# One scalar step of the second normalisation moved ahead of two VectorE instructions in beat 5 of a Hyena and gated-FFN kernel

## The reference

```python
u  = x @ in_proj_w.T + in_proj_b            # 1536 columns, then a causal convolution of 3 taps
x0, x1, v = split(short_conv(u))
v  = fftconv(v * x1, k, filter_bias)        # long convolution; k comes from a small network
x  = layernorm(x + (v * x0) @ out_proj_w.T + out_proj_b)
h  = silu(x @ Wg.T) * (x @ Wu.T)            # 1408 hidden columns, dequantised integer weights
x  = layernorm(x + h @ Wd.T)
```

## Time and profile before

| | before |
|---|---|
| runs | 1001.90, 1002.41, 1002.76 us (median 1002.41) |
| profiled execution | 1001.72 us, span 999.9 us |
| TensorE busy | 972.3 us, 97% of the span |
| VectorE, GpSimd, ScalarE busy | 734.2, 570.5, 426.7 us |
| granted TensorE clock | 0.996 of 2.4 GHz as a mean |

### The profile page before, as it was taken

One profiled execution on the slowest core, in us unless ns is written; L12 is line 12 of the kernel. 1 busy time (PEld: TensorE's weight loads), 2 busy tenths in 40 slices (PEclk: granted clock), 3 DMA queues, 4 the chain that ended last, 5 costly groups with the idle time before them and its releaser, 6 DMA issues.

```text
span 999.9 us, 17201 instructions
## 1 busy us (share of the span) xinstructions
PE 972.3 (97%) x6188; PEld 761.7 (76%) x6188; DVE 734.2 (73%) x1345; ACT 426.7 (43%) x929; POOL 570.5 (57%) x628
## 2 busy tenths in 40 slices
PE   7999999999999999999999999999999999999996
PEld 5578777778777777778777787777877777787774
DVE  6598776868777787777878777876877777686454
ACT  4675534333353434434443343443335343434242
POOL 4589673755646476464656647465654747565210
PEclk9999999999999999999999999999999999999998
DMA  8654101121122101221102211112111110101100
GB/s 248 202 178 122 39 1 23 21 64 23 43 43 55 31 2 43 43 64 22 32 12 43 64 23 43 27 26 55 22 43 22 43 22 1 44 1 44 43 22 22
DMA packets 98952, 47.96 MB, mean 48 GB/s; under 512 B 80048, under 2 KB 84784, under 8 KB 98868
## 3 DMA queue, kind: packets, MB, share of 16 engines
q1 hardware_dynamic: 98370, 46.79, 18.0%
q10 hardware_dynamic: 498, 0.08, 0.0%
HBM read 32.17 MB, written 8.39 MB: 41 GB/s over the span
## 4 chain that ended last, share of the span: by engine, by line
PE 69%; DVE 13%; issue 6%; ACT 5%; POOL 4%; DMA 1%; ACTq 0%; POOLq 0%; SPq 0%; DVEq 0%
PE gate_up L1132 11%; PE gate_up L1133 11%; PE bank L992 9%; PE bank L994 9%; PE bank L993 9%; PE down L1144 5%; PE down L1145 5%; PE bank L1092 4%; DVE hid_lo L982 2%; DVE tmp L903 2%; ACT cx L675 2%; DVE cx L876 2%; PE bank L1067 1%; ACT x L700 1%; DVE cx L879 1%
## 5 line engine op out<-in xcount | busy, mean ns | idle before, releaser
L762 POOL TENSOR_TENSOR acc<-acc,tmp 128x256 f32<-128x256 f32 x160 | 123.3, 770 | 148.9 <-DVE tmp L903 136.9
L903 DVE TENSOR_TENSOR tmp<-spectrum,filt 128x512 f32<-128x512 f32 x256 | 172.6, 680 | 0.4 <-PE spectrum L994 0.4
L1132 PE MATMUL gate_up<-x2T_hi,wg_sb 128*128 128x256 f16 x704 | 163.4, 273 | 0.0
L1133 PE MATMUL gate_up<-x2T_lo,wu_sb 128*128 128x256 f16 x704 | 163.3, 273 | 0.0
L1133 PE MATMUL gate_up<-x2T_lo,wg_sb 128*128 128x256 f16 x704 | 163.3, 273 | 0.0
L1132 PE MATMUL gate_up<-x2T_hi,wu_sb 128*128 128x256 f16 x704 | 163.2, 273 | 0.0
L726 ACT ACTIVATE hid<-gate_up,gate_scale 128x256 f32<-128x256 f32 x176 | 82.7, 470 | 184.9 <-PE gate_up L1133 184.8
L756 POOL TENSOR_TENSOR acc<-acc,tmp 128x512 f32<-128x512 f32 x96 | 126.3, 1315 | 48.5 <-DVE tmp L903 48.0
L992 PE MATMUL bank<-xT_hi,win_hi 128*128 128x512 f32 x360 | 149.5, 415 | 1.4 <-POOL win_lo L744 1.2
L994 PE MATMUL bank<-xT_hi,win_lo 128*128 128x512 f32 x360 | 143.4, 398 | 0.0
L993 PE MATMUL bank<-xT_lo,win_hi 128*128 128x512 f32 x360 | 143.0, 397 | 0.0
(11 more groups left out here) (170 smaller groups left out, 1831.5 us busy)
## 6 DMA issues: line engine op xcount, KB each, us to landing
x<-in_x SPq DMA_DIRECT2D x28, 256.0 KB, 2.8
out<-x SPq DMA_DIRECT2D x28, 256.0 KB, 2.1
xstage<-in_x SPq DMA_DIRECT2D x96, 64.0 KB, 2.5
xstage<-in_x SPq DMA_DIRECT2D x12, 256.0 KB, 3.9
x<-in_win SPq DMA_DIRECT2D x12, 256.0 KB, 4.9
acc<-in_decay SPq DMA_DIRECT2D x4, 256.0 KB
x<-in_wout SPq DMA_DIRECT2D x4, 256.0 KB, 2.8
x2T_hi<-in_wu SPq DMA_DIRECT2D x4, 256.0 KB, 4.2
```

The lines of the kernel that those rows point to most:

```text
L762: G.tensor_tensor(acc[:, i, 0, :], acc[:, i, 0, :], t[:, 1, :], ALU.subtract)
L903: TT(dst, spectrum[j % 2][:, :, :], k_part, ALU.mult).then_inc(made_done, 1)
L1132: mm(dst, w[:, kb, rows(q)], x2T_hi[:, kb, ts], start=kb == 0, stop=False)
L1133: last = mm(dst, w[:, kb, rows(q)], x2T_lo[:, kb, ts], start=False, stop=kb == CB - 1)
```

## The change

In the passes in which beat 5 has both a half to finish (`done`) and a unit (`u`), the step `norm LN2` stands behind `hhi` of the unit, where it stood behind the second part of `mul`, `hlo` and `dn`. Passes n = 4 to 18 have both; n = 19 has no unit and stays.

```diff
     if u:
         steps += [("hmul", *u), ("hhi", *u)]
+        if beat == 5 and done:
+            steps += [("norm", LN2, n - 4)]
...
     if beat == 5 and done:
-        steps += [("norm", LN2, n - 4)]
+        if not u:
+            steps += [("norm", LN2, n - 4)]
         steps += [("store", n - 4, 0), ("store", n - 4, 1)]
```

## The result

| | before | after |
|---|---|---|
| median of 6 runs | 1002.15 us | 995.25 us (994.19 to 996.12) |
| ratio, 95% interval | | 0.9932 (0.9920 to 0.9944) |
| profiled execution, span | 1001.72, 999.9 us | 995.0, 993.2 us |

The account below looks back on a forecast made before the run. The prediction took TensorE's instructions plus its waits to bound the kernel. Steady passes -6.74, pass 16 +2.33 and pass 17 -0.56 gave -4.97 us, from 1002.41 to 997.4 us, range 994.8 to 1000.3.

Parts of the forecast that it names:

- The chain: Steady passes: TensorE's `op` waits for convolution L879, behind ScalarE's L675, behind normalisation L700, behind `shift`; all twelve waits go.
- The size of that term: Steady passes 4 to 15: twelve waits of TensorE removed in full, -6.74 us.
- every wait really costs 0.17 us more than its bracket: TensorE's waits: down products start 0.21 us apart but show as 0.38 long, so 12 x 0.17 joins 4.7 us.
- Hold of `shift`: VectorE, steady passes: moved `shift` lasts 0.58 us (bounds 0.15 and 1.23), delaying `mul` part 1 at no cost to TensorE.
- Pass 16: n = 16: `shift` waits for late `rstd` with `mul` part 1 and `hlo` queued behind, so `fw(15, 3)` starts late, +2.33 us.
- Pass 17: n = 17: normalisation of m = 13, its stores and reload come earlier, shortening TensorE's wait for `hlo`, -0.56 us.
- The sum: Whole kernel: -6.74 + 2.33 - 0.56 = -4.97 us, forecast 997.4 us, chance 0.50.
- The lower clock: Rival: TensorE's clock drops behind the new stall in pass 16, costing 1.70 us, 999.1 us; chance 0.21.
- Pass 16 costs nothing: Rival: GpSimd's backlog shrinks and `rstd` is early in pass 16, -7.3 us, 995.1 us; chance 0.09.
- The waits: Rival: another release takes over for `op`, half of the twelve waits left, -1.6 us, 1000.8 us; chance 0.12.
- The slower rival: `shift` holds `mul` part 1 until `fw(n-1, 3)` waits; with 4.5 us of hold +8.2 us, 1010.6 us; chance 0.03.

Follow-up runs that it names:

- e1: Against the kernel before: `shift` moved in the steady passes alone (n = 4 to 15), passes 16 and 17 in the old order; 994.73 us, ratio 0.9927.
- e4: Against the kernel before: `shift` of all fourteen places moved up by one instruction only, between `mul` part 1 and `hlo`; 994.62 us, ratio 0.9927.
- e3: Against the kernel before: VectorE's order kept, ScalarE's normalisation L700 put behind the convolution L675 in the steady passes; 994.02 us, ratio 0.9924.
- e8: e3 with `shift` of m = 13 (pass 17) moved as well; 994.39 us, ratio 0.9918 to the kernel before.
- e9: e1 with four extra VectorE instructions, output unused, behind each of the twelve moved `shift`s, 2.4 us of hold; 993.78 us, ratio 0.9920.
- e10: e1 with seven extra VectorE instructions, output unused, behind each of the twelve moved `shift`s, 4.2 us of hold; 1006.37 us, ratio 1.0049.
- e2: Against the kernel before: `shift` of m = 12 (pass 16) alone moved; 1004.49 us, ratio 1.0024.
- e7: Changed kernel, all fourteen places moved, with GpSimd computing `rstd` of m = 12 ahead of two additions; 993.78 us, ratio 0.9909.
- e6: Changed kernel with the old order for m = 12 (pass 16) alone; 993.66 us, ratio 0.9911.
- e11: The changed kernel measured and profiled once more, beside e12 on one chip; 995.52 us, ratio 0.9932.
- e12: The kernel of e7 measured and profiled once more, beside e11; 993.39 us, ratio 0.9915.
- e5: Against the kernel before: `shift` of m = 13 (pass 17) alone moved, one profile; 1002.84 us.

## Why the prediction was right, and where it was off

- **The chain.** TensorE's twelve waits came from L675 queued behind L700 behind `shift`. Shown from three sides: by moving `shift` (e1), by moving it less (e4), and by not moving it and reordering ScalarE (e3, e8). e1, e4 and e8 give -8.0 us in the steady stretch; of e3 there are only the times, with a ratio like theirs.
- **The size of that term** was forecast as 4.7 + 12 x 0.17 = 6.74 us and measured as 8.0. The step that failed is "every wait really costs 0.17 us more than its bracket". I took the loss up to the start of the first product and left out that this product then takes 0.33 us to the next one where 0.24 is usual. By the loads the gain is 0.77 us in pass 4, 0.81 to 0.83 in passes 5, 7, 9, 11 and 13, and 0.51 to 0.53 in the other six, 8.0 together.
- **Hold of `shift`**: taken 0.58 us out of a range from 0.15 to 1.23, measured 0.55 to 0.56 in eleven steady passes and 1.14 in the first. Its cost of nothing is right: 2.4 us more of it is free (e9), 4.2 us is not (e10). With `fw` 0.86 late behind 4.2 us of hold the cover is 3.3 us, against 3.4 in the prediction, which left out the 0.14 us from the end of `mul` to `fw`. One reading there was off: a `shift` that starts at 492.22 and ends near 494.0 lasts 1.78 us, 0.55 more than the upper bound of 1.23 and not "a little"; the bank would then be free 0.2 us ahead and not 0.8. In e4 `shift` does end there (490.73, or 494.0 in before's times), and the waits are gone all the same.
- **Pass 16**: forecast +2.33, measured +2.37 to +2.39, for the stated reason (e2, e7). What the sum did not have is what follows: 0.80 us come back at two waits of TensorE for `hlo` (0.41 at 913.7 and 0.39 at 920.3 us before). The expectations of e2 and e6 say that the stall gives them back, and the traces bear that out. The first of the two waits ends a chain on VectorE that begins when GpSimd's L779 releases L918; before, VectorE and TensorE:

```profile
907.32 0.69 DVE L918 TENSOR_TENSOR xstage<-bank,xstage 128x512 f32<-128x512 f32 x1 [4.05 <-POOL xstage L779]
...
912.95 0.72 DVE L982 TENSOR_TENSOR hid_lo<-hid,hid_hi 128x256 f16<-128x256 f32 x1
...
913.72 0.39 PE L1144 MATMUL down<-wd_sb,hid_hi 128*128 128x512 bf16 x1
```

TensorE's stall does not delay L918, so TensorE comes later to an `hlo` that is ready. In e4, where the stall is 1.26 us, this `hlo` ends at 905.88 us, to 0.01 where it was (913.67 before, less the 7.78 by which TensorE is ahead until pass 16), and the down product starts 1.0 us behind it without a wait:

```profile
905.16 0.72 DVE L984 TENSOR_TENSOR hid_lo<-hid,hid_hi 128x256 f16<-128x256 f32 x1
...
906.89 0.38 PE L1146 MATMUL down<-wd_sb,hid_hi 128*128 128x512 bf16 x1
```

With a stall of 2.38 us L918 stands where it was too, to 0.06 us (changed kernel, e2, e11). In e7 and e12 TensorE is only 0.45 us late, but L918 comes 0.58 us earlier (906.74 for 907.32 in before's times), and the two together again exceed 0.80. So at most the 0.80 us of these two waits can come back, whatever the stall. That some 0.25 us are lost there in e1, e5, e6, e8 and e9 has another cause: GpSimd's `rstd` of m = 12 lasts 0.98 us in these five and 0.71 before and in e10, and `shift` and the two waits end about 0.27 us later. It starts within 0.02 us of VectorE's `hlo`, which lasts 0.41 us in the five, 0.47 before and 0.46 in e10, so the same two instructions meet each time with a different outcome, in e5 too, where nothing ahead of them is changed.

- **Pass 17**: forecast -0.56; -0.44 and -0.35 in the changed kernel, and 0.49 between the means with and without it. The sign holds, and the chain up to the reload with 0.67 us (e5); the size of what reaches TensorE is blurred by the transfer.
- **The sum** by the profile: +0.15 - 8.01 + 2.37 - 0.80 - 0.44 = -6.73, and the spans differ by 6.7. The forecast of -4.97 is short by 1.3 in the first term and 0.8 in the second, and both errors go the same way. That the time still lies 0.45 us inside the range owes something to luck: its lower end of 994.8 was set for another case, a free pass 16, which did not come.
- **The rivals.** The lower clock did not come: behind the stall of 2.1 to 2.2 us the granted clock stayed at 1.00 in the three profiles that have it (changed kernel, e2, e11). "Pass 16 costs nothing" gave nearly the right time (995.1) for the wrong reason. The waits did not come back, and no other release took over (TensorE has no wait from 180 to 880 us). The slower rival's hold did not occur; e10 makes it by hand, and its 4.2 us of hold put the steady stretch 5.3 us above before.

The best kernels are e7/e12 and e6, with ratios 0.9909 and 0.9915, and 0.9911: the change with the place of m = 12 either repaired or left alone. They are not told apart from each other.

## What to carry to other kernels

When TensorE waits for a bank, follow the wait back through each queue to the first instruction that did not need the one ahead of it: here a 128x2 instruction behind 2.1 us of unrelated work on one engine, or equally a normalisation ahead of a convolution on another, and either order mends it. When the same reordering is made in all passes of a pipeline, look at the filling and emptying passes one by one: the twelve steady ones gave 8.0 us, and a single one, in which the input came late, took 2.4 back (1.6 net, as TensorE then caught up with two waits further on). And count a wait to the second matmul behind it.

## What the runs showed of the hardware

A wait of 2.2 us in pass 1 was followed by half clock in before's profile, and the same wait in the changed kernel's profile, also 2.2 us, was not. Windows of the changed kernel, clock in the third column from the end, then the second one in e11, the same kernel profiled again, where the wait was 2.25 us:

```profile
109.00:112.00 3.00, 1.21 (x9) 1.03 (x10) 1.45 (x4) 2.53 (x4) 2.70 (x4) 1.00 0.01 3
112.00:114.00 2.00, 2.00 (x12) 1.61 (x11) 1.98 (x4) 0.60 (x1) 1.25 (x2) 1.00 0.04 8
...
112.00:114.00 2.00, 2.00 (x7) 1.52 (x6) 2.00 (x5) 0.00 (x0) 0.56 (x2) 0.50 0.00 0
```

Of the thirteen profiles (all but e3's), each with this wait of 2.2 us, twelve have a granted clock of 0.50 to 0.78 from 112 to 114 us, and this one has 1.00. So for a pause of this length at this place the drop varies from one execution to the next, and a forecast can only give it a chance. Its price can be read too: the changed kernel's loads lie 1.43 us behind before's at 109.5 us and 0.15 at 120 us, so the full clock gave 1.28 us there, where the prediction's rival counted 1.70. The +0.15 of the table's first column is thus 1.43 us of loading less 1.28 of clock.

The stretch of `shift` by a running GpSimd product or addition was exact wherever I read it: `shift`, 0.15 us long by itself, lasted until the GpSimd instruction ended, 0.01 to 0.02 us behind it, whether that made it 0.56, 0.68 or 1.2 us long. The Trainium skill ("SBUF — State Buffer", section "SBUF: two separate sides") states this as a lock held for a whole instruction, and these rows agree with it. GpSimd's `rstd` behaves otherwise: in pass 16 before, an `hlo` that ran beside it (897.95 to 898.42) ended 0.23 us ahead of it (898.65), which a lock held for all of the 0.71 us that the trace shows for `rstd` would not allow.
